# Graph attention on one core: the low part of the probabilities is taken two chunks back, the values three chunks back

## The chip, the cores and the metric

The kernel runs on 1 core of one Trainium2 chip. The metric is the device time of the launch in microseconds (us). Beside it there is one profiled execution, from which all durations come.

## What is computed

For 128 graphs of 128 nodes with 384 features, 12 heads of 32 features:

```python
h = maximum(layernorm(x), 0)
q, k, v = h @ Wq + bq, h @ Wk + bk, h @ Wv + bv          # split into 12 heads
scores = q @ k.T / sqrt(32) + beta * adj                 # per graph and head, 128 x 128
scores = where(adj > 0, scores, -9e15)
out = x + softmax(scores) @ v
```

## The kernel before

**Steps and slots.** A step takes 4 graphs (512 nodes), and there are 32. Each engine has its own instruction stream, and all five are written in the same frame: steps, and in each step 12 slots `u`. A step projects its own four graphs (q, k, v), prepares the normalised input of the next step, and does the attention of the step before. A chunk is one graph and four heads, so that a step has 12 chunks, one scored in each slot, 3 slots behind (`LAG`). A 33rd step, without projections, does what is left. The function `chunk(s, par, u, behind)` names the chunk that was scored `behind` slots ago.

**A chunk n on its way**, with the names used below:

- S: `scores` (L458), TensorE, four matmuls 128x128 into the one bank `ps_s`. It waits until B of n-1 is done.
- B: `bias_scores` (L638), VectorE, four instructions that add the mask, negate and take the row minimum (`neg_max`), each with a read of the accumulator. It waits for S, and for the exponentials of n-2, whose input it overwrites.
- E: `exps` (L523), ScalarE, four exponentials, each after its part of B.
- T: `turn_probs` (L466), TensorE, four transposes in f32 into `ps_t`, two banks in turn. It waits for E of n, and for L of n-2, which reads the same bank.
- H: `p_high` (L548), ScalarE, the transposed probabilities rounded to f16. It waits for T and for V of n-2, whose operand it overwrites.
- L: `p_low` (L644), VectorE, the bank minus H: the low part, in f16. It waits for H.
- V: `values_of` (L481 to L483), TensorE, 12 matmuls, probabilities (high and low) times values. It waits for L; with the first chunk of a graph also for the values' split on GpSimd and for a free output bank.
- After the third chunk of a graph VectorE inverts the sums (L654) and scales the output (L659), GpSimd adds x (L336), SyncE stores.

**The projections** are cut into pieces, one for each slot (`piece`, L437): q, k of 9 matmuls with 512 columns a unit, v of 9 with 384 columns, and three `turn` units (L417), transposes of the next step's input. They run over three banks. A unit's result is taken in two parts: ScalarE the high part (L543, L538, or L530 for hT) in the slot in which the unit ends, VectorE the low part (L619, or L609 for hT) in the slot after. A unit may start when the bank's earlier tenant is emptied: `bank_free`.

**The order in a slot** that scores chunk n is:

- TensorE: S(n), T(n-1), piece, V(n-2).
- ScalarE: E(n), H(n-1), high parts of the slot's units.
- VectorE: B(n), low parts of the units of the slot before, inversion, statistics (L586, L592; slots 0 and 1), scaling, mask (L598 in slot 4, L603 in slot 7), L(n-1).

The slots of the pieces, by `PIECES`: seven matmuls of q or k in slots 0, 1, 3, 4 and 7, eight in slot 2; slot 5 has turn 0 and five of k 1; slot 6 four of k 1, turn 1 and two of k 2; slot 8 turn 2 and seven of v 0; slots 9 to 11 ten, nine and ten of v. The first matmul of k 2 (slot 6) needs the bank of turn 0, thus its low part, which VectorE makes in slot 6.

Of the kernel before, what the change touches and what calls it, by code (L numbers as in the profile page):

```python
# [23 lines left out]
def graph_attention_kernel(nc, x, adj, wq, bq, wk, bk, wv, bv, beta, out):  # L24
# [6 lines left out]
    STEPS = GRAPHS // G  # L31
    TOK = G * N
    SLOTS = G * CH
    CHUNKS = STEPS * SLOTS

    LAG = CH
# [48 lines left out]
    with ExitStack() as ctx:  # L85
# [115 lines left out]
        def wait(eng, s, value):  # L201

            if value > 0:
                eng.wait_ge(s, value)
# [6 lines left out]
        def chunk(s, par, u, behind):  # L211

            v = u - LAG - behind
            back = 2 if v < 0 else 1
            n = SLOTS * (s - 1) + v
            if v >= SLOTS or (not 0 <= n < CHUNKS):
                return None
            return n, s - back, par if back == 2 else 1 - par, v % SLOTS
# [171 lines left out]
        def _(pe):  # L390
# [50 lines left out]
            def piece(s, par, u, ahead):  # L441

                for o, first, end in PIECES[u]:
                    if UNITS[o][0] != "turn":
                        project(s, par, o, first, end)
                    elif ahead:
                        bank_free(s, par, o)
                        turn(s + 1, ps_p[BANK[par][o]], UNITS[o][1])

            def scores(n, g, gp, v, odd):  # L450

                j, c = v // CH, v % CH
                if v == 0:
                    pe.wait_ge(q_in, 16 * 3 * HPC * (g + 1))
                    pe.wait_ge(k_in, 16 * 3 * HPC * (g + 1))
                wait(pe, biased_done, HPC * n)
                for i in range(HPC):
                    mm = pe.matmul(ps_s[:, i * N:(i + 1) * N], q_st[0:STACK, gp, i, c, j * N:(j + 1) * N],  # L458
                                   k_st[0:STACK, gp, i, c, j * N:(j + 1) * N], start=True, stop=True)
                mm.then_inc(scores_done, 1)  # L460

            def turn_probs(n, odd):
                pe.wait_ge(exp_done, HPC * (n + 1))
                wait(pe, p_low_done, n - 1)
                for i in range(HPC):
                    mm = pe.transpose(ps_t[odd][:, i * N:(i + 1) * N], probs[:, odd, i, :], ident[:])  # L466
                mm.then_inc(turned, 1)

            def values_of(n, g, gp, v, odd):

                j, c = v // CH, v % CH
                if c == 0:
                    wait(pe, scaled, G * g + j - 1)
                    pe.wait_ge(v_split, G * g + j + 1)
                pe.wait_ge(p_low_done, n + 1)
                for i in range(HPC):
                    h = c * HPC + i
                    o = ps_o[j % 2][:, h * VW:(h + 1) * VW]
                    high, low = pT[:, odd, 0, i, :], pT[:, odd, 1, i, :]
                    first, second = v1[:, gp, j, h, :], v2[:, gp, j, h, :]  # L480
                    pe.matmul(o, high, first, start=True, stop=False)  # L481
                    pe.matmul(o, low, first, start=False, stop=False)  # L482
                    mm = pe.matmul(o[:, 0:HD], high, second, start=False, stop=True)  # L483
                mm.then_inc(pv_done, 1)

            def step(s, par):
                proj, ahead = 0 <= s <= STEPS - 1, 0 <= s <= STEPS - 2
                for u in range(SLOTS + (LAG + 2 if s == STEPS else 0)):
                    scored, turning, valued = (chunk(s, par, u, behind) for behind in range(3))
                    if scored:  # L490
                        scores(*scored, (u - LAG) % 2)
                    if turning:
                        turn_probs(turning[0], (u - LAG - 1) % 2)
                    if proj:
                        piece(s, par, u, ahead)
                    if valued:
                        values_of(*valued, (u - LAG) % 2)

            pe.wait_ge(consts_set, 3)
            for n in range(3):  # L500
# [81 lines left out]
        def _(dve):  # L582
            def moments(s, par, j):
                wait(dve, x_in[par], 8 * (s - par) + 16)
                wait(dve, var_done, G * (s - 1) + j + 1)
                dve.bn_stats(stats[:, j, :], xs[:, par, j, :]).then_inc(stats_done, 1)  # L586
# [7 lines left out]
            def mask_unlinked(s, par):  # L594

                dve.wait_ge(adj_in, 16 * (s + 1))
                wait(dve, biased_done, HPC * SLOTS * (s - 1))
                dve.tensor_scalar(mask[:, par], adjs[:], 0.0, MASKED, ALU.is_le, ALU.mult).then_inc(unlinked, 1)  # L598
# [23 lines left out]
            def low_parts(s, par, u, ahead):  # L622

                for o in ENDED[u]:
                    if UNITS[o][0] in ("q", "k"):
                        low_part(s, par, o)
                    elif UNITS[o][0] == "turn" and ahead:
                        turn_low(s + 1, 1 - par, ps_p[BANK[par][o]], UNITS[o][1])

            def bias_scores(n, g, gp, v, odd):  # L630

                dve.wait_ge(scores_done, n + 1)
                wait(dve, exp_done, HPC * (n - 1))
                if v == 0:
                    dve.wait_ge(mask_done, g + 1)
                dve.nop(nofuse=True)
                for i in range(HPC):
                    dve.tensor_tensor_reduce(out=biased[:, odd, i, :], in0=ps_s[:, i * N:(i + 1) * N],  # L638
                                             in1=mask[:, gp, v // CH, :], scale=-1.0, scalar=3.0e38, op0=ALU.add,
                                             op1=ALU.min, accum_out=neg_max[:, odd, i:i + 1]).then_inc(biased_done, 1)  # L640

            def p_low(n, odd):
                dve.wait_ge(p_high_done, n + 1)
                dve.tensor_tensor(pT[:, odd, 1], ps_t[odd][:].rearrange("p (h q) -> p h q", q=N), pT[:, odd, 0],  # L644
                                  ALU.subtract).then_inc(p_low_done, 1)
# [4 lines left out]
            def invert_sums(g, j):  # L650

                dve.wait_ge(pv_done, CH * (G * g + j + 1))
                wait(dve, scaled, G * g + j - 1)
                dve.reciprocal(inv_sum[:, j % 2, :], outputs(j)[:, :, HD]).then_inc(inverted, 1)  # L654

            def scale_out(g, j):
                dve.wait_ge(inverted, G * g + j + 1)
                wait(dve, stored[j % 2], 16 * (G // 2 * g + j // 2))
                dve.tensor_tensor(on[:, j % 2, :].rearrange("p (h d) -> p h d", d=HD), outputs(j)[:, :, 0:HD],  # L659
                                  inv_sum[:, j % 2, :].rearrange("p (h o) -> p h o", o=1).broadcast_to([P, HEADS, HD]),  # L660
                                  ALU.mult).then_inc(scaled, 1)

            def step(s, par):
                proj, ahead = 0 <= s <= STEPS - 1, 0 <= s <= STEPS - 2
                for u in range(SLOTS + (LAG + 3 if s == STEPS else 0)):
                    scored, turning, _, valued = (chunk(s, par, u, behind) for behind in range(4))
                    ended = valued is not None and valued[3] % CH == CH - 1
                    if scored:
                        bias_scores(*scored, (u - LAG) % 2)
                    if u >= 1 and proj:  # L670
                        low_parts(s, par, u - 1, ahead)
                    if u == 0 and s >= 1:
                        low_parts(s - 1, 1 - par, SLOTS - 1, s <= STEPS - 1)
                    if ended:
                        invert_sums(valued[1], valued[3] // CH)
                    if ahead and u < 2:
                        for j in range(2 * u, 2 * u + 2):
                            moments(s + 1, 1 - par, j)
                    if ended:
                        scale_out(valued[1], valued[3] // CH)  # L680
                    if proj and u == 4:
                        mask_unlinked(s, par)
                    if proj and u == 7:
                        mask_linked(s, par)
                    if ahead and u < 2:
                        for j in range(2 * u, 2 * u + 2):
                            variance(s + 1, j)
                    if turning:
                        p_low(turning[0], (u - LAG - 1) % 2)

            for j in range(G):
                moments(0, 0, j)
# [86 lines left out]
```

## Time and profile before

| | |
|---|---|
| time, median of 3 runs | 1162.81 us (1161.45 to 1163.67) |
| profiled execution, its own time | 1164.11 us |
| its span, first to last instruction | 1162.2 us |
| TensorE (PE) busy | 1070.8 us, 92% |
| VectorE (DVE) busy | 979.4 us, 84% |
| ScalarE (ACT) busy | 892.2 us, 77% |
| GpSimd (POOL) busy | 567.8 us, 49% |
| mean granted TensorE clock | 0.976 |
| DMA | 138.79 MB, mean 119 GB/s |

The busy shares are shares of the span. Matmuls are pipelined, and each is listed with its full latency, so that TensorE's busy time holds overlaps; its real pace is read from the starts of its instructions. The same holds in a smaller way for VectorE and ScalarE, where an instruction starts some hundredths of a us before the one ahead ends. Therefore durations below are mostly differences of starts.

### The profile page before, as it was taken

What the parts mean: (1) busy time and instruction counts of PE and PEld (TensorE: products, weight loads), DVE (VectorE), ACT (ScalarE), POOL (GpSimd) and SP (SyncE); (2) the same over time, 40 slices, a digit from 0 to 9 for tenths busy, and PEclk for the clock granted to TensorE, in tenths of its full rate; (3) what the DMA queues carried; (4) which work ended last, traced back from release to release, by engine and by line L of the source; (5) the groups of instructions that cost most, each with busy time, mean ns of one, the idle gap of its engine ahead of it and who ended that gap; (6) DMA issues with size and microseconds to landing.
All of it is one profiled execution on the core that took longest, in us unless ns stands there. A gap on an engine that the chain in (4) does not pass through costs nothing. (4 is left out here: it accounts for less than half of the span.)

```text
span 1162.2 us, 33776 instructions
## 1 busy us (share of the span) xinstructions
PE 1070.8 (92%) x10959; PEld 713.0 (61%) x10959; DVE 979.4 (84%) x4343; ACT 892.2 (77%) x2343; POOL 567.8 (49%) x756
## 2 busy tenths in 40 slices
PE   4899999999999999999999999999999999999986
PEld 1366666666666666666666666666666666666654
DVE  6588988888988888898888898888889888889765
ACT  2378887778788787888787877888888878887865
POOL 3744555544455544455554445554445555444431
PEclk9999999999999999999999999999999999999965
DMA  4454434455444455444445444445544444543320
GB/s 144 118 133 122 116 101 123 126 146 137 114 104 120 120 140 147 113 123 104 115 132 146 130 122 102 118 123 139 146 114 115 110 119 130 147 129 95 98 69 28
DMA packets 91038, 138.79 MB, mean 119 GB/s; under 512 B 15600, under 2 KB 66288, under 8 KB 90864
## 3 DMA queue, kind: packets, MB, share of 16 engines
q1 hardware_dynamic: 90336, 135.85, 43.5%
q8 instruction: 88, 1.44, 0.5%
q14 instruction: 86, 0.70, 0.2%
q10 hardware_dynamic: 528, 0.79, 0.2%
HBM read 35.91 MB, written 25.17 MB: 53 GB/s over the span
## 5 line engine op out<-in xcount | busy, mean ns | idle before, releaser
L523 ACT ACTIVATE probs<-biased,neg_max 128x128 f32<-128x128 f32 x1536 | 493.5, 392 | 225.3 <-DVE neg_max L638 223.2
L437 PE MATMUL ps_p<-hT,w 128*128 128x512 f16 x1728 | 423.8, 382 | 30.1 <-DVE hT L609 22.0
L644 DVE TENSOR_TENSOR pT<-ps_t,pT 128x512 f16<-128x512 f32 x384 | 264.4, 689 | 146.9 <-ACT pT L548 143.5
L638 DVE CUSTOM_DVE_ANT_0 biased<-ps_s,mask 128x128 f32<-128x128 f32 x1536 | 351.7, 286 | 3.8 <-PE ps_s L458 2.9
L336 POOL TENSOR_TENSOR on<-on,xb 128x384 f32<-128x384 f32 x128 | 127.7, 997 | 417.7 <-DVE on L659 417.7
L466 PE MATMUL ps_t<-ident,probs 128*128 128x128 f32 x1536 | 255.0, 290 | 32.4 <-ACT probs L523 12.1
L437 PEld LDWEIGHTS ps_p<-hT,w 128*128 128x128 f16 x1728 | 166.2, 98 | 185.2 <-DVE hT L609 29.3
L548 ACT ACTIVATE pT<-ps_t 128x512 f16<-128x512 f32 x384 | 221.1, 576 | 0.7 <-PE ps_t L466 0.7
L466 PEld LDWEIGHTS ps_t<-ident,probs 128*128 128x128 f32 x1536 | 165.3, 144 | 82.8 <-ACT probs L523 81.3
L437 PE MATMUL ps_p<-w,hT 128*128 128x384 f16 x1152 | 207.6, 326 | 0.0
L481 PEld LDWEIGHTS ps_o<-v,pT 128*128 128x128 f16 x1536 | 132.2, 97 | 46.1 <-DVE pT L644 6.6
L481 PE MATMUL ps_o<-v,pT 128*128 128x33 f16 x1536 | 156.8, 179 | 3.2 <-DVE pT L644 2.3
L483 PE MATMUL ps_o<-v,pT 128*128 128x32 f16 x1536 | 155.7, 177 | 0.0
L482 PE MATMUL ps_o<-v,pT 128*128 128x33 f16 x1536 | 155.6, 178 | 0.0
L458 PE MATMUL ps_s<-k_st,q_st 96*128 96x128 f16 x1536 | 150.2, 221 | 5.4 <-DVE neg_max L638 4.3
L437 PEld LDWEIGHTS ps_p<-w,hT 128*128 128x128 f16 x1152 | 112.7, 98 | 59.7
L482 PEld LDWEIGHTS ps_o<-v,pT 128*128 128x128 f16 x1536 | 125.2, 97 | 36.7
L321 POOL TENSOR_TENSOR xb<-xs,bv_row 128x384 f32<-128x384 f32 x128 | 127.3, 1006 | 8.9 <-POOL on L336 0.4
L638 DVE DVE_READ_ACCUMULATOR2_ANT neg_max<- 128x1 f32 x1536 | 129.0, 84 | 0.0
L483 PEld LDWEIGHTS ps_o<-v,pT 128*128 128x128 f16 x1536 | 124.1, 96 | 0.0
L328 POOL CAST v<-v_f 128x384 f16<-128x384 f32 x128 | 64.8, 506 | 111.8 <-issue 102.7
L330 POOL TENSOR_TENSOR v<-v_f,v 128x384 f16<-128x384 f32 x128 | 113.6, 887 | 10.3
(62 smaller groups left out, 1044.4 us busy)
## 6 DMA issues: line engine op xcount, KB each, us to landing
q_st<-qT SPq DMA_DIRECT2D x384, 96.0 KB, 2.2
k_st<-kT SPq DMA_DIRECT2D x384, 96.0 KB, 2.2
out<-on SPq DMA_DIRECT2D x128, 192.0 KB, 2.1
xs<-in_x SPq DMA_DIRECT2D x31, 768.0 KB, 4.7
adjs<-in_adj SPq DMA_DIRECT2D x32, 256.0 KB, 4.9
xs<-in_x ACTq DMA_DIRECT2D x1, 768.0 KB, 7.3
k_st<-in_L_gnn_Wq SPq DMA_DIRECT2D x1, 576.0 KB, 5.6
k_st<-in_L_gnn_Wk SPq DMA_DIRECT2D x1, 576.0 KB, 9.4
```

The costliest lines, as they stand in the source:

```text
L321: pool.tensor_tensor(xb[:, par, j, :], xs[:, par, j, :], bv_row[:], ALU.add).then_inc(xb_done, 1)
L336: pool.tensor_tensor(on[:, j % 2, :], on[:, j % 2, :], xb[:, par, j, :], ALU.add).then_inc(added, 1)
L437: mm = pe.matmul(dst, stationary, moving, start=m == 0, stop=m == MMS - 1)
L458: mm = pe.matmul(ps_s[:, i * N:(i + 1) * N], q_st[0:STACK, gp, i, c, j * N:(j + 1) * N], k_st[0:STACK, gp, i, c, j * N:(j + 1) * N], start ...
L466: mm = pe.transpose(ps_t[odd][:, i * N:(i + 1) * N], probs[:, odd, i, :], ident[:])
L481: pe.matmul(o, high, first, start=True, stop=False)
L482: pe.matmul(o, low, first, start=False, stop=False)
L483: mm = pe.matmul(o[:, 0:HD], high, second, start=False, stop=True)
L523: act.activation(probs[:, odd, i, :], biased[:, odd, i, :], ACT.Exp, bias=neg_max[:, odd, i:i + 1], scale=-1.0).then_inc(exp_done, 1)
L548: act.activation(pT[:, odd, 0], ps_t[odd][:].rearrange("p (h q) -> p h q", q=N), ACT.Copy).then_inc(p_high_done, 1)
L638: dve.tensor_tensor_reduce(out=biased[:, odd, i, :], in0=ps_s[:, i * N:(i + 1) * N], in1=mask[:, gp, v // CH, :], scale=-1.0, scalar=3.0e3 ...
L644: dve.tensor_tensor(pT[:, odd, 1], ps_t[odd][:].rearrange("p (h q) -> p h q", q=N), pT[:, odd, 0], ALU.subtract).then_inc(p_low_done, 1)
```

## The change

On VectorE L is taken of the chunk n-2 instead of n-1, and stands directly behind B(n) instead of at the end of the slot. On TensorE V is taken of the chunk n-3 instead of n-2, and stands between S and T instead of behind the piece. ScalarE, GpSimd and SyncE keep their instructions and order. The last step has one more slot on TensorE. No buffer and no instruction is added or removed.

```diff
--- before.py
+++ after.py
@@ -485,16 +485,16 @@
 
             def step(s, par):
                 proj, ahead = 0 <= s <= STEPS - 1, 0 <= s <= STEPS - 2
-                for u in range(SLOTS + (LAG + 2 if s == STEPS else 0)):
-                    scored, turning, valued = (chunk(s, par, u, behind) for behind in range(3))
+                for u in range(SLOTS + (LAG + 3 if s == STEPS else 0)):
+                    scored, turning, valued = (chunk(s, par, u, behind) for behind in (0, 1, 3))
                     if scored:
                         scores(*scored, (u - LAG) % 2)
+                    if valued:
+                        values_of(*valued, (u - LAG - 3) % 2)
                     if turning:
                         turn_probs(turning[0], (u - LAG - 1) % 2)
                     if proj:
                         piece(s, par, u, ahead)
-                    if valued:
-                        values_of(*valued, (u - LAG) % 2)
 
             pe.wait_ge(consts_set, 3)
             for n in range(3):
@@ -663,10 +663,12 @@
             def step(s, par):
                 proj, ahead = 0 <= s <= STEPS - 1, 0 <= s <= STEPS - 2
                 for u in range(SLOTS + (LAG + 3 if s == STEPS else 0)):
-                    scored, turning, _, valued = (chunk(s, par, u, behind) for behind in range(4))
+                    scored, turned_late, valued = (chunk(s, par, u, behind) for behind in (0, 2, 3))
                     ended = valued is not None and valued[3] % CH == CH - 1
                     if scored:
                         bias_scores(*scored, (u - LAG) % 2)
+                    if turned_late:
+                        p_low(turned_late[0], (u - LAG) % 2)
                     if u >= 1 and proj:
                         low_parts(s, par, u - 1, ahead)
                     if u == 0 and s >= 1:
@@ -685,8 +687,6 @@
                     if ahead and u < 2:
                         for j in range(2 * u, 2 * u + 2):
                             variance(s + 1, j)
-                    if turning:
-                        p_low(turning[0], (u - LAG - 1) % 2)
 
             for j in range(G):
                 moments(0, 0, j)
```

TensorE, slot 9 of a middle step (S is L458, T L466, the piece L437, V L481 to L483), before:

```order
L458 MATMUL ps_s<-k_st,q_st 128x128 [waits biased_done]
L458 MATMUL ps_s<-k_st,q_st 128x128 x3
L466 MATMUL ps_t<-ident,probs 128x128 [waits p_low_done,exp_done]
L466 MATMUL ps_t<-ident,probs 128x128 x3
L437 MATMUL ps_p<-w,hT 128x384 x2
L437 MATMUL ps_p<-w,hT 128x384 [waits qk_low]
L437 MATMUL ps_p<-w,hT 128x384 x7
L481 MATMUL ps_o<-v,pT 128x33 [waits p_low_done]
L482 MATMUL ps_o<-v,pT 128x33
L483 MATMUL ps_o<-v,pT 128x32
```

The same stretch now (the nine rows left out are the rest of V):

```order
L458 MATMUL ps_s<-k_st,q_st 128x128 [waits biased_done]
L458 MATMUL ps_s<-k_st,q_st 128x128 x3
L481 MATMUL ps_o<-v,pT 128x33 [waits p_low_done,v_split,scaled]
L482 MATMUL ps_o<-v,pT 128x33
L483 MATMUL ps_o<-v,pT 128x32
...
L466 MATMUL ps_t<-ident,probs 128x128 [waits p_low_done,exp_done]
L466 MATMUL ps_t<-ident,probs 128x128 x3
L437 MATMUL ps_p<-w,hT 128x384 x2
L437 MATMUL ps_p<-w,hT 128x384 [waits qk_low]
L437 MATMUL ps_p<-w,hT 128x384 x7
```

V, with its wait for `p_low_done`, now stands behind S and ahead of T; before it stood behind the piece.

VectorE, around slot 4 of a middle step (B is L638 with its accumulator reads, L is L644, the low part of qT L619, the first mask L598), before:

```order
L644 TENSOR_TENSOR pT<-ps_t,pT 128x512 [waits p_high_done]
L638 ISA biased,neg_max<-ps_s,mask 128x128 [waits scores_done,exp_done]
L638 ISA neg_max 128x1
...
L619 SCALAR_TENSOR_TENSOR qT<-ps_p,bias_qk,qT 128x512 [waits qk_high]
L598 TENSOR_SCALAR mask<-adjs 128x512 [waits biased_done,adj_in]
L644 TENSOR_TENSOR pT<-ps_t,pT 128x512 [waits p_high_done]
L638 ISA biased,neg_max<-ps_s,mask 128x128 [waits scores_done,exp_done]
```

The same stretch now:

```order
L638 ISA biased,neg_max<-ps_s,mask 128x128 [waits scores_done,exp_done]
L638 ISA neg_max 128x1
...
L644 TENSOR_TENSOR pT<-ps_t,pT 128x512 [waits p_high_done]
L619 SCALAR_TENSOR_TENSOR qT<-ps_p,bias_qk,qT 128x512 [waits qk_high]
L598 TENSOR_SCALAR mask<-adjs 128x512 [waits biased_done,adj_in]
L638 ISA biased,neg_max<-ps_s,mask 128x128 [waits scores_done,exp_done]
```

Between two B stood the slot's other work and then L with its wait for `p_high_done`; now L stands right behind B, and nothing that waits for a fresh H stands ahead of the next B.

## Rows read from the trace of the kernel before

**Rows 1.** Waits of the whole run: in total us, how often, longest.

```profile
ACT probs L523 <- DVE neg_max L638: 223.2, 355, 2.1
...
DVE pT L644 <- ACT pT L548: 143.5, 204, 1.6
...
PEld ps_t L466 <- ACT probs L523: 81.3, 279, 1.1
```

**Rows 2.** Timeline behind the last projection: start, duration, engine, instructions, [idle before <-releaser].

```profile
1131.22 1.28 ACT L523 ACTIVATE probs<-biased,neg_max 128x128 f32<-128x128 f32 x4 [1.02 <-DVE neg_max L638]
...
1132.41 0.58 ACT L548 ACTIVATE pT<-ps_t 128x512 f16<-128x512 f32 x1
...
1133.02 0.69 DVE L644 TENSOR_TENSOR pT<-ps_t,pT 128x512 f16<-128x512 f32 x1 [1.26 <-ACT pT L548]
1133.63 0.28 DVE L638 CUSTOM_DVE_ANT_0 biased<-ps_s,mask 128x128 f32<-128x128 f32 x1
...
1134.01 1.28 ACT L523 ACTIVATE probs<-biased,neg_max 128x128 f32<-128x128 f32 x4 [1.02 <-DVE neg_max L638]
...
1135.35 1.11 PE L466 MATMUL ps_t<-ident,probs 128*128 128x128 f32 x4
```

**Rows 3.** Timeline, TensorE over a slot without a wait.

```profile
618.51 0.38 PE L458 MATMUL ps_s<-k_st,q_st 96*128 96x128 f16 x4
618.74 0.61 PE L466 MATMUL ps_t<-ident,probs 128*128 128x128 f32 x4
619.18 1.67 PE L437 MATMUL ps_p<-hT,w 128*128 128x512 f16 x7
...
620.69 0.18 PE L481 MATMUL ps_o<-v,pT 128*128 128x33 f16 x1
...
620.99 0.38 PE L458 MATMUL ps_s<-k_st,q_st 96*128 96x128 f16 x4
```

**Rows 4.** Timeline, VectorE's kinds of work, and the groups by line: the first mask.

```profile
602.98 1.02 DVE L586 BATCH_NORM_STATS2 stats<-xs 128x6 f32<-128x384 f32 x2
...
604.33 0.69 DVE L644 TENSOR_TENSOR pT<-ps_t,pT 128x512 f16<-128x512 f32 x1
...
604.94 0.28 DVE L638 CUSTOM_DVE_ANT_0 biased<-ps_s,mask 128x128 f32<-128x128 f32 x1
...
605.78 0.75 DVE L619 SCALAR_TENSOR_TENSOR qT<-ps_p,bias_qk,qT 128x512 f16<-128x512 f32 x1
...
606.44 0.22 DVE L654 RECIPROCAL inv_sum<-ps_o 128x12 f32<-128x12 f32 x1
...
607.17 0.68 DVE L644 TENSOR_TENSOR pT<-ps_t,pT 128x512 f16<-128x512 f32 x1
...
620.59 0.68 DVE L609 SCALAR_TENSOR_TENSOR hT<-ps_p,hT 128x512 f16<-128x512 f32 x1
621.18 0.74 DVE L603 SCALAR_TENSOR_TENSOR mask<-adjs,beta_col,mask 128x512 f32<-128x512 f32 x1
621.84 0.69 DVE L644 TENSOR_TENSOR pT<-ps_t,pT 128x512 f16<-128x512 f32 x1
...
L598 DVE TENSOR_SCALAR mask<-adjs 128x512 f32<-128x512 f32 x32 | 14.2, 444 | 0.0
```

**Rows 5.** Timeline, low part of hT and the projection that waits for it.

```profile
617.02 0.69 DVE L609 SCALAR_TENSOR_TENSOR hT<-ps_p,hT 128x512 f16<-128x512 f32 x1
...
617.77 0.60 PE L437 MATMUL ps_p<-hT,w 128*128 128x512 f16 x2 [0.74 <-DVE hT L609]
```

**Rows 6.** Timeline, the first chunk.

```profile
58.05 0.38 PE L458 MATMUL ps_s<-k_st,q_st 96*128 96x128 f16 x4 [1.02 <-DMA k_st<-kT]
...
58.62 0.29 DVE L638 CUSTOM_DVE_ANT_0 biased<-ps_s,mask 128x128 f32<-128x128 f32 x1 [2.88 <-PE ps_s L458]
...
58.96 1.28 ACT L523 ACTIVATE probs<-biased,neg_max 128x128 f32<-128x128 f32 x4 [2.06 <-DVE neg_max L638]
```

**Rows 7.** Stretch behind the last projection: busy us of each engine, PEclk, DMA share, GB/s.

```profile
1130.00:1162.00 32.00, 21.46 (x204) 14.23 (x203) 18.05 (x91) 16.68 (x47) 4.78 (x5) 0.50 0.09 32
```


## The prediction

> **What bounds the kernel now.** I read the waits first [rows 1]. ScalarE waits 223.2 us before E for VectorE's row minimum, VectorE 143.5 us before L for H, and TensorE's weight loads 81.3 us, 279 times, before T for E. Three engines that wait for each other in a ring: the question is which ring closes. The timeline behind the last projection shows it bare [rows 2]. E starts at 1131.22, H at 1132.41, L at 1133.02, the next B at 1133.63, the next E at 1134.01: E 1.19, H 0.61, L 0.61, first part of B 0.38, in sum 2.79 us a chunk, each starting when the one ahead lets it. E(n-1), H(n-2), L(n-2), B(n), E(n): the only reason for the step from L to B is VectorE's order, since B reads nothing that L writes. TensorE has little to do there and the period is still 2.79, so it is a ring of ScalarE and VectorE alone.
>
> With projections the same ring holds. The first E starts at 58.96 [rows 6]; the E at 1131.22 [rows 2] is 375 chunks later. Six of these are behind the last projection, at 2.79; the other 369 take 1072.26 - 16.7 = 1055.5 us, 2.86 each, or 34.33 a step. TensorE's own pace is lower. In a slot without a wait S takes 0.23, T 0.44, seven matmuls of 512 columns 1.51 (0.216 each, so 0.162 for 384 columns) and V 0.30 [rows 3]; a turn is four f32 transposes like T, 0.44. With the pieces of the 12 slots: 2.48 in slots 0, 1, 3, 4, 7; 2.70 in 2 and 6; 2.49 in 5; 2.54, 2.59, 2.43, 2.59 in 8 to 11. Sum 30.44 a step, 3.9 less than the step takes. I call that TensorE's floor.
>
> VectorE's work, by starts [rows 4]: B 0.84 (604.94 to 605.78), L 0.61, a low part of q or k 0.66, of hT 0.59, inversion with scaling 0.73, statistics 1.35, masks 0.44 and 0.66. By slot 0 to 11: 2.80, 2.80, 2.84, 2.11, 2.55, 2.84, 2.04, 3.36, 2.84, 2.04, 1.45, 2.18; sum 29.85. So its mean is just under TensorE's, but in six slots it has more to do.
>
> **The change, part by part.** Nothing is removed or added, so the work stays 30.44 and 29.85.
>
> 1. L out of the way of B. B(n) now waits for S(n) and for VectorE's other work. The link L to B of the ring is gone; L(n-2) comes after B(n), a full slot after H(n-2), so it should not wait: the 143.5 us should all but vanish, and so should most of the 223.2.
>
> 2. V between S and T. It gives E 0.30 us more before T needs it, but V itself is now needed at 0.23 into the slot, and T, the piece and the next S are queued behind it. V(n-3) needs L(n-3), which VectorE makes in the slot before, behind B. H(n-1) waits for V(n-3), which stands ahead of T(n-1) anyway: no new cost.
>
> 3. What TensorE then waits for. I lay the slots out. B starts 0.57 after S at the earliest [rows 6]; V is released 0.84 + 0.75 after B starts (0.75 is from the start of a 512-column VectorE instruction to the matmul that waits for it [rows 5]); T is released 0.38 + 1.34 after B starts (the 1.34 is E at 1134.01 to T at 1135.35 [rows 2]). TensorE's slot starts at 0 in slot 0, VectorE's B at 0.57. VectorE's B then starts behind TensorE's slot by 0.57, 0.89, 1.21, 1.35, 0.98, 0.82, 1.17 in slots 0 to 6. V waits where the lag in the slot before, plus 1.59, passes that slot's length plus 0.23: only in slot 4, by 0.23 (1.35 + 1.59 = 2.94 against 2.71). In slot 6 k 2 needs hT's low part, now behind B and L: 1.17 + 1.45 + 0.75 = 3.37 after the slot's start, against 2.27 where TensorE gets there. Wait 1.10. Before, it was 0.74 by the row [rows 5]. This wait lets VectorE catch up: lag 0.57 in slot 7, 1.45 in 8 (slot 7 has 3.36 of work), 1.75 in 9, 0.93 in 10, 0.57 in 11. V waits 0.27 in slot 9 and 0.25 in slot 10. T's condition (lag + 1.72 against the slot's length + 0.53) is never the later one. A step is 30.44 + 0.23 + 1.10 + 0.27 + 0.25 = 32.29 us.
>
> 4. The sum. 34.33 - 32.29 = 2.04 a step, times 369/12 = 30.75 steps: 62.7 us. The last step with projections has no turns and no statistics: TensorE needs 3 x 0.44 less and the wait of 1.10 is gone, while its old pace is the ring's 2.79; I put 2 us more.
>
> 5. Behind the last projection, 15 chunks at 2.79. TensorE is at the granted clock 0.50 there, 1.2 GHz [rows 7], so S, V and T cost at most twice the 0.97 of [rows 3]: 1.94. VectorE needs (3 x 1.45 + 0.73)/3 = 1.69, ScalarE 1.19 + 0.48 (E, and H when it doesn't wait) = 1.67. Between 1.69 and 1.94 and nearer the upper, since V waits for L and the scaling comes in bursts: 1.9. Gain 15 x 0.89 = 13.3. The Trainium skill (TensorE: Matmul & The Clock Gate, Part 1) says that activity releases TensorE's throttle. The row agrees that the clock is low where TensorE is sparse; by that rule the denser tail could stay at 2.4 GHz, and then VectorE's 1.69 would hold and the total be 3 us lower. I keep the 0.50 of the row.
>
> The extra slot on TensorE costs nothing: the last V waits for the last L either way.
>
> What no row shows is the handing over from V's short matmuls to T's f32 weight loads. The nearest rows are S to T, 0.23 with nothing added, and T's start after a wait. Below nothing is excluded by in-order work; above I take 0.05 a slot, 0.6 a step, 18 us. I take 0 and keep 18 for the range.
>
> Sum: 62.7 + 2 + 13.3 = 78 us off the profiled execution's 1164.1, which gives 1086; the median of the runs is 1.3 lower, so **1085**.
>
> **Rivals.**
>
> - **TensorE's floor.** If VectorE's real lag is smaller than my sums (0.57 was read once, at the first chunk), V never waits and only hT's wait of 1.10 stays: 31.54 a step, 2.79 x 30.75 + 15 = 101 off, **1062**. For it: V's three waits are small. Against: six slots of VectorE are longer than TensorE's.
> - **No slack between the engines.** If each slot costs the longer of the two engines, 2.80, 2.80, 2.84, 2.48, 2.55, 2.84, 2.70, 3.36, 2.84, 2.59, 2.43, 2.59 = 32.82, with hT's wait 33.92 a step: 0.41 x 30.75 + 15 = 28 off, **1135**. For it: V at the slot's head has only L's slack. Against: S needs B only by the slot's end, 0.3 us after B is done even at lag 1.35. A part of this rival, and the 18 us above, are the way to the upper end.
> - **Slower: V's wait becomes the ring.** V(n), T(n+2) 0.44, piece 1.51, S to B 0.57, B 0.84, L to V 0.75, with V's 0.30: 4.41 us from V(n) to V(n+2), two chunks, plus what VectorE has to do ahead of B(n+4). It decides from 2 x 2.86 = 5.72 up, when 1.31 more lies ahead. The mean other work of a slot is (29.85 - 12 x 1.45)/12 = 1.04, giving 5.45; the longest, slot 7's, is 1.91, giving 6.32. If every second pair met that, a chunk took 2.94, 0.08 x 369 = 30 more, less 13 for the tail: **1181**. Against: 1.91 comes once a step.
> - **No change.** The two buffers of pT and ps_t are the true bound, and the wait moves from L to V and H. The Trainium skill (Perfetto Trace Analysis, Identifying Performance Opportunities) says that a bubble that repeats can mean too few buffers; no buffer is added here. Against: the rows name another engine's result, and the ring of [rows 2] closes through the order alone. **1163**.
>
> **Chances.** Forecast 0.60 (alone: 1070 to 1102), floor 0.17, no slack 0.15, slower 0.04, no change 0.04. Range 1060 to 1116: the floor with its small variations is in, of the no-slack case the milder half. A difference under 0.2% (2.3 us) can't be told from none. Faster 0.92, same 0.04, slower 0.04.
>
> **What the profile after should show.** L's wait for H near nothing; E's wait for the row minimum well under half of 223; T's wait for E nearly gone, and in its place V waiting for L in slots 4, 9 and 10, some 90 times by 0.2 to 0.3; hT's wait in slot 6 longer, near 1.1; 32.3 us between like points of two steps; under 2 us a chunk behind the last projection. Wrong it would be if VectorE still idled over 1 us a slot, if V waited in most slots, or if a wait for k_st's or q_st's transfer, with less time now, appeared at a step's first S.

## The result, and the profile after

The changed kernel takes 1079.64 us (median of 4 runs, 1078.93 to 1080.68); the kernel before 1162.28 us in the same comparison. The ratio is 0.9289, 95% interval 0.9273 to 0.9305. Forecast were 1085 us, range 1060 to 1116.

| | before | after |
|---|---|---|
| span of the profiled execution | 1162.2 us | 1077.4 us |
| TensorE busy | 1070.8 us, 92% | 1020.8 us, 95% |
| VectorE busy | 979.4 us, 84% | 967.6 us, 90% |
| ScalarE busy | 892.2 us, 77% | 884.5 us, 82% |
| mean granted TensorE clock | 0.976 | 0.992 |

The work is the same; the span is 84.8 us shorter. First the waits of the whole run after (waiter, whom for, total us, times, longest):

```profile
ACT probs L523 <- DVE neg_max L638: 115.5, 217, 1.4
DVE biased L638 <- PE ps_s L458: 74.5, 100, 1.7
...
PEld ps_p L437 <- DVE hT L609: 26.1, 31, 1.1
...
PEld ps_o L481 <- DVE pT L644: 5.9, 15, 1.2
...
DVE pT L644 <- ACT pT L548: 0.9, 1, 0.9
...
PEld ps_t L466 <- ACT probs L523: 0.3, 1, 0.3
```

These answer to [rows 1]. VectorE's wait for H fell from 143.5 us to 0.9, so L no longer waits. T's wait for E fell from 81.3 us to 0.3. ScalarE's wait for the row minimum is 115.5 us, half of the 223.2: it is not a bound now, only the time that ScalarE has over. VectorE waits for S instead, 74.5 us (2.9 before): in the light slots it has caught up with TensorE.

One step, on TensorE (start, duration, operation; slot 2, S of slot 3, then slots 6, 9 and 10, then slot 2 of the next step):

```profile
599.81 0.39 PE L458 MATMUL ps_s<-k_st,q_st 96*128 96x128 f16 x4
...
600.34 0.64 PE L466 MATMUL ps_t<-ident,probs 128*128 128x128 f32 x4
600.81 1.89 PE L437 MATMUL ps_p<-hT,w 128*128 128x512 f16 x8
602.54 0.39 PE L458 MATMUL ps_s<-k_st,q_st 96*128 96x128 f16 x4
...
610.09 0.39 PE L458 MATMUL ps_s<-k_st,q_st 96*128 96x128 f16 x4
...
611.95 0.60 PE L417 MATMUL ps_p<-ident,hn 128*128 128x128 f32 x4
613.17 0.61 PE L437 MATMUL ps_p<-hT,w 128*128 128x512 f16 x2 [0.62 <-DVE hT L609]
...
618.71 0.39 PE L458 MATMUL ps_s<-k_st,q_st 96*128 96x128 f16 x4
619.23 0.18 PE L481 MATMUL ps_o<-v,pT 128*128 128x33 f16 x1
...
621.62 0.39 PE L458 MATMUL ps_s<-k_st,q_st 96*128 96x128 f16 x4
621.97 0.19 PE L481 MATMUL ps_o<-v,pT 128*128 128x33 f16 x1
...
631.87 0.39 PE L458 MATMUL ps_s<-k_st,q_st 96*128 96x128 f16 x4
```

VectorE's B in slots 3, 6 and 9 of the same step:

```profile
603.63 0.28 DVE L638 CUSTOM_DVE_ANT_0 biased<-ps_s,mask 128x128 f32<-128x128 f32 x1
...
610.99 0.28 DVE L638 CUSTOM_DVE_ANT_0 biased<-ps_s,mask 128x128 f32<-128x128 f32 x1
...
620.38 0.28 DVE L638 CUSTOM_DVE_ANT_0 biased<-ps_s,mask 128x128 f32<-128x128 f32 x1
```

From S of slot 2 at 599.81 to the next at 631.87 are 32.06 us, where 34.33 were. TensorE reaches k 2 (the last projection unit of slot 6, behind turn 1) at 611.95 + 0.44 = 612.39 and waits until 613.17, 0.78 us. V starts 0.52 after S in slot 9 (618.71 to 619.23) and 0.35 after in slot 10, where 0.22 is the pace without a wait: waits of 0.30 and 0.13. T to the piece is 0.47 (600.34 to 600.81), not the 0.44 of [rows 3]. B starts 1.09 behind S in slot 3 (602.54 to 603.63), 0.90 in slot 6 (610.09 to 610.99) and 1.67 in slot 9 (618.71 to 620.38).

Where the 84.8 us are, by the exponentials. After: the first chunk, the first behind the last projection, and the fourteenth after that.

```profile
58.42 1.28 ACT L523 ACTIVATE probs<-biased,neg_max 128x128 f32<-128x128 f32 x4 [0.88 <-DVE neg_max L638]
...
1043.11 1.28 ACT L523 ACTIVATE probs<-biased,neg_max 128x128 f32<-128x128 f32 x4
...
1068.39 1.28 ACT L523 ACTIVATE probs<-biased,neg_max 128x128 f32<-128x128 f32 x4
```

Before, where the first chunk is in [rows 6]:

```profile
1114.49 1.28 ACT L523 ACTIVATE probs<-biased,neg_max 128x128 f32<-128x128 f32 x4 [0.27 <-DVE neg_max L638]
...
1153.53 1.28 ACT L523 ACTIVATE probs<-biased,neg_max 128x128 f32<-128x128 f32 x4 [1.02 <-DVE neg_max L638]
```

369 chunks took 1055.5 us and take 984.7 (58.42 to 1043.11, 32.02 a step): 70.8 us. The next 14 took 39.04 and take 25.28: 13.8 us. The rest, 0.2, is at the two ends.

### The profile page after: what moved, and what is told of

The parts are those of the page before. It is cut to its first block and busy times, and to the rows that moved or that the text cites. A ratio compares the mean times of both kernels' runs of the same rounds, so it can differ in the third digit from the quotient of the medians.

```text
span 1077.4 us, 33776 instructions
## 1 busy us (share of the span) xinstructions
PE 1020.8 (95%) x10959; PEld 709.7 (66%) x10959; DVE 967.6 (90%) x4343; ACT 884.5 (82%) x2343; POOL 567.5 (53%) x756
## 5 line engine op out<-in xcount | busy, mean ns | idle before, releaser
L523 ACT ACTIVATE probs<-biased,neg_max 128x128 f32<-128x128 f32 x1536 | 490.5, 390 | 146.9 <-DVE neg_max L638 115.5
L437 PE MATMUL ps_p<-hT,w 128*128 128x512 f16 x1728 | 423.5, 382 | 23.9 <-DVE hT L609 18.7
L638 DVE CUSTOM_DVE_ANT_0 biased<-ps_s,mask 128x128 f32<-128x128 f32 x1536 | 353.5, 286 | 75.8 <-PE ps_s L458 74.5
L437 PEld LDWEIGHTS ps_p<-hT,w 128*128 128x128 f16 x1728 | 167.5, 98 | 175.7 <-DVE hT L609 26.1
L644 DVE TENSOR_TENSOR pT<-ps_t,pT 128x512 f16<-128x512 f32 x384 | 263.3, 686 | 0.9 <-ACT pT L548 0.9
L466 PE MATMUL ps_t<-ident,probs 128*128 128x128 f32 x1536 | 245.4, 283 | 0.1
L437 PE MATMUL ps_p<-w,hT 128*128 128x384 f16 x1152 | 207.6, 326 | 0.0
L458 PEld LDWEIGHTS ps_s<-k_st,q_st 96*128 96x128 f16 x1536 | 117.5, 97 | 81.3 <-DVE neg_max L638 6.9
L481 PE MATMUL ps_o<-v,pT 128*128 128x33 f16 x1536 | 157.1, 179 | 8.9 <-DVE pT L644 5.2
L466 PEld LDWEIGHTS ps_t<-ident,probs 128*128 128x128 f32 x1536 | 161.7, 141 | 0.3 <-ACT probs L523 0.3
L483 PE MATMUL ps_o<-v,pT 128*128 128x32 f16 x1536 | 155.2, 177 | 0.0
L458 PE MATMUL ps_s<-k_st,q_st 96*128 96x128 f16 x1536 | 149.4, 219 | 3.7 <-DVE neg_max L638 2.4
L437 PEld LDWEIGHTS ps_p<-w,hT 128*128 128x128 f16 x1152 | 112.7, 98 | 59.7
L481 PEld LDWEIGHTS ps_o<-v,pT 128*128 128x128 f16 x1536 | 130.1, 96 | 20.5 <-issue 10.7
L638 DVE DVE_READ_ACCUMULATOR2_ANT neg_max<- 128x1 f32 x1536 | 127.5, 83 | 0.3
L483 PEld LDWEIGHTS ps_o<-v,pT 128*128 128x128 f16 x1536 | 123.7, 96 | 0.0
```

What stands on the lines that cost most here:

```text
L437: mm = pe.matmul(dst, stationary, moving, start=m == 0, stop=m == MMS - 1)
L523: act.activation(probs[:, odd, i, :], biased[:, odd, i, :], ACT.Exp, bias=neg_max[:, odd, i:i + 1], scale=-1.0).then_inc(exp_done, 1)
```

## The experiments

Each kernel is the changed one or the one before, with one thing altered. Times are medians; ratios are to the kernel before, run beside it on the same chip (1161.65 us beside the values behind the transposes, the changed kernel once more and the operation in slot 7; 1161.53 beside the first four; 1161.40 beside the other four).

### The two moves apart, and the two places

**The values alone.** VectorE's stream is that of the kernel before, TensorE's that of the changed kernel.

```diff
-                    scored, turned_late, valued = (chunk(s, par, u, behind) for behind in (0, 2, 3))
+                    scored, turning, _, valued = (chunk(s, par, u, behind) for behind in range(4))
...
-                    if turned_late:
-                        p_low(turned_late[0], (u - LAG) % 2)
...
+                    if turning:
+                        p_low(turning[0], (u - LAG - 1) % 2)
```

> The values alone are moved (three chunks back, between scores and transposes); VectorE keeps the low part of the last chunk at the end of its slot, so the ring of ScalarE and VectorE (exponentials, high part, low part, next masked scores: 2.79 us a chunk) is whole. Theory (the order of VectorE was the bound): about 1162 us, within 6, still 2.79 us a chunk behind the last projection, and VectorE still waits some 140 us for the high part. Rival (the gain came from the 0.30 us that the values give the exponentials before the transposes need them): under 1120 us.

Measured: 1157.96 us, ratio 0.9969 (0.9958 to 0.9981). The ring is whole, and so is the time, all but 3.6 us: the rival is out. Its exponentials behind the last projection (ScalarE, timeline):

```profile
1124.88 1.28 ACT L523 ACTIVATE probs<-biased,neg_max 128x128 f32<-128x128 f32 x4 [1.03 <-DVE neg_max L638]
...
1127.67 1.28 ACT L523 ACTIVATE probs<-biased,neg_max 128x128 f32<-128x128 f32 x4 [1.02 <-DVE neg_max L638]
```

Three of its waits:

```profile
DVE pT L644 <- ACT pT L548: 142.0, 204, 1.5
...
PEld ps_s L458 <- DVE neg_max L638: 95.1, 260, 1.6
...
PEld ps_t L466 <- ACT probs L523: 3.7, 8, 1.1
```

Still 2.79 us a chunk, and 142.0 us of L waiting for H. T's wait for E did vanish (3.7 us, from 81.3), just as the 0.30 us of V ahead of it would have it, and TensorE waits 95.1 us at S for B instead (5.7 before). A wait of TensorE that disappears tells nothing if the ring that made it doesn't run through TensorE.

**The low part alone.** VectorE's stream is the changed one, TensorE's that of the kernel before.

```diff
-                for u in range(SLOTS + (LAG + 3 if s == STEPS else 0)):
-                    scored, turning, valued = (chunk(s, par, u, behind) for behind in (0, 1, 3))
+                for u in range(SLOTS + (LAG + 2 if s == STEPS else 0)):
+                    scored, turning, valued = (chunk(s, par, u, behind) for behind in range(3))
...
-                    if valued:
-                        values_of(*valued, (u - LAG - 3) % 2)
                     if turning:
                         turn_probs(turning[0], (u - LAG - 1) % 2)
                     if proj:
                         piece(s, par, u, ahead)
+                    if valued:
+                        values_of(*valued, (u - LAG) % 2)
```

> The low part alone is moved behind the masked scores, of the chunk but one back; the values keep their place behind the piece and are of two chunks back, so they need a low part that VectorE makes in the same slot. Theory: the ring is broken, but TensorE now waits at the end of its slot (lag of VectorE + 0.84 + 0.75 against 2.18), by hand 33.5 us a step against 32.06 now, and 2.46 us a chunk behind the last projection against 1.8: about 1134 us. Rival (the move of VectorE's low part is all of the change, the values' move a detail): within 10 us of 1080.

Measured: 1130.08 us, ratio 0.9732 (0.9703 to 0.9760). So 31 us come from moving L alone, which takes the link from L to B out of the ring, and the other 51 of the whole change from where V stands. The rival, within 10 us of 1080, is out. By its exponentials the 369 chunks take 1022.6 us, 32.9 less than before, but the 14 behind the last projection only 1.0 less (38.04 us, 2.72 each, where 2.46 were forecast): there V waits for L of its own slot, and the next S stands behind V. V is now the instruction that waits:

```profile
PEld ps_o L481 <- DVE pT L644: 98.7, 226, 1.6
...
PE ps_o L481 <- DVE pT L644: 40.0, 53, 1.3
```

**The low part at the end of VectorE's slot**, of the chunk but one back as in the change.

```diff
-                    if turned_late:
-                        p_low(turned_late[0], (u - LAG) % 2)
...
                             variance(s + 1, j)
+                    if turned_late:
+                        p_low(turned_late[0], (u - LAG) % 2)
```

> As the changed kernel, but VectorE takes the low part (of the chunk but one back, as changed) at the end of its slot, not behind the masked scores. If only the distance to the high part matters (rival), the ring is broken all the same and it stays within 10 us of 1080. Theory of the lags: the values at the head of TensorE's slot need this low part 0.14 us after the end of VectorE's slot, so that a slot takes VectorE's work + 0.48 us wherever that is longer: 36.4 us a step, about 1210 us, slower than before.

Measured: 1160.27 us, ratio 0.9990 (0.9979 to 1.0001): in sum the gain is gone, though the ring is broken (of L's wait for H only 1.0 us is left, once). The rival is out; the theory's direction is right and its size wrong, 1210 forecast. The head of slot 8 (TensorE's S and V, VectorE's L and B):

```profile
626.70 0.39 PE L458 MATMUL ps_s<-k_st,q_st 96*128 96x128 f16 x4
...
627.52 0.68 DVE L644 TENSOR_TENSOR pT<-ps_t,pT 128x512 f16<-128x512 f32 x1
...
628.12 0.28 DVE L638 CUSTOM_DVE_ANT_0 biased<-ps_s,mask 128x128 f32<-128x128 f32 x1
...
628.25 0.19 PE L481 MATMUL ps_o<-v,pT 128*128 128x33 f16 x1 [1.17 <-DVE pT L644]
```

V stands 1.55 us behind S (626.70 to 628.25), and starts 0.73 after L does. My sum charged each of VectorE's long slots to TensorE in full. But a slot that V has made longer gives VectorE that time back: the wait in slot t + 1 is VectorE's end of slot t + 0.14, less the start of slot t + 1, less 0.23, with the wait of slot t in that start. Done so, with the prediction's own numbers, a step has 3.98 us of waits and takes 34.42; the trace has 34.63 in the mean of the 369 chunks (59.50 to 1124.49). The unchanged time hides two parts, by the first exponential behind the last projection and the fourteenth after it:

```profile
1124.49 1.28 ACT L523 ACTIVATE probs<-biased,neg_max 128x128 f32<-128x128 f32 x4
...
1150.51 1.27 ACT L523 ACTIVATE probs<-biased,neg_max 128x128 f32<-128x128 f32 x4
```

The 369 chunks take 1065.0 us, 9.5 more than before; the next 14 take 26.02, 13.0 less. So the broken ring shows where VectorE has little other work, and in the steps L's late place takes it back.

**The values behind the piece**, of three chunks back as in the change.

```diff
-                    if valued:
-                        values_of(*valued, (u - LAG - 3) % 2)
                     if turning:
                         turn_probs(turning[0], (u - LAG - 1) % 2)
                     if proj:
                         piece(s, par, u, ahead)
+                    if valued:
+                        values_of(*valued, (u - LAG - 3) % 2)
```

> As the changed kernel, but TensorE takes the values of three chunks back behind the piece instead of between scores and transposes. The values then never wait for the low part (0.43 us a step won), but the high part waits for them until TensorE's slot ends, ScalarE's high parts and the next exponentials stand behind it, and the transposes lose 0.30 us of slack: by hand 0.5 to 0.8 us a step more, about 1100 us. Rival (the place within the slot is free, only the distance counts): 1066 to 1075 us.

Measured: 1104.61 us, ratio 0.9512 (0.9485 to 0.9540). Of the 51 us, then, the greater distance of V gives 25 and its place in the slot the other 25. The rival (1075 at most) is out. H now waits for V, since V reads the buffer that H overwrites, and T waits behind that:

```profile
ACT pT L548 <- PE ps_o L483: 110.6, 198, 1.5
...
...
PEld ps_t L466 <- ACT probs L523: 34.6, 97, 0.8
```

**The values behind the transposes.**

```diff
-                    if valued:
-                        values_of(*valued, (u - LAG - 3) % 2)
                     if turning:
                         turn_probs(turning[0], (u - LAG - 1) % 2)
+                    if valued:
+                        values_of(*valued, (u - LAG - 3) % 2)
                     if proj:
```

> As the changed kernel, but the values of three chunks back stand behind the transposes, ahead of the piece. They no longer wait for the low part (0.43 us a step), but the transposes are 0.30 us earlier in the slot and wait for the exponentials where VectorE is late: by the lags of the changed kernel's trace 0.07 in slot 4, 0.33 in slot 9, 0.2 in slot 10. Theory: about 0.2 us a step more, 1080 to 1088 us. Rival (the values' wait for the low part is the dearer of the two): 1066 to 1074 us.

Measured: 1084.50 us, ratio 0.9335 (0.9320 to 0.9351); the changed kernel beside it gave 0.9293 (0.9279 to 0.9306). So the place ahead of T is worth 5 us, and the rival is out. T and V in slot 7 of a middle step, where neither waits:

```profile
616.75 0.61 PE L466 MATMUL ps_t<-ident,probs 128*128 128x128 f32 x4
...
617.19 0.18 PE L481 MATMUL ps_o<-v,pT 128*128 128x33 f16 x1
```

Behind S, as in the kernel before, T takes 0.44 (616.75 to 617.19); directly behind V, in the changed kernel, it takes 0.47.

**The changed kernel once more.**

> The changed kernel once more, on the chip of the two runs above: 1079.6 us, within 2.

Measured: 1079.39 us.

### Is VectorE the bound, and where?

**An operation more in slot 10, and in slot 7**, read by nobody:

```diff
                     if turned_late:
                         p_low(turned_late[0], (u - LAG) % 2)
+                    if proj and u == 10:
+                        dve.tensor_tensor(spare[:], b_row[:], b_row[:], ALU.add)
```

The counterpart has `u == 7`. Both allocate the tile `spare`, 128x768 in f32.

> The changed kernel with one idle VectorE operation more in slot 10 of each step (the bias rows, 768 columns, added to themselves into a spare tile, read by nobody; about 0.8 us). VectorE waits 0.83 us for scores there. Theory of the lags (VectorE isn't the bound as a whole, only in the slots after its long ones): it costs under 0.1 us a step, 1079 to 1083 us. Rival (VectorE, at 90% busy, is the bound): 0.8 us a step, 1104 us. The same operation in slot 7 is to follow as its counterpart.

> The same idle VectorE operation as before (768 columns), now in slot 7, VectorE's longest. In slot 10 it took 1.45 us in the one place read and cost nothing. Theory of the lags: here it makes VectorE late for slots 8 and 9 and shows in full as TensorE's waits, its own duration a step (0.8 us without company of GpSimd, up to 1.45): 25 to 45 us more, 1104 to 1125 us. Rival (VectorE's work has slack wherever it stands): under 1085 us.

Measured: 1079.64 us (ratio 0.9293, 0.9275 to 0.9312) in slot 10, 1106.38 us (0.9524, 0.9509 to 0.9538) in slot 7. The operation itself, by its tile (count, then the least, the median and the greatest duration in ns), in slot 10:

```profile
L674 DVE TENSOR_TENSOR spare<-b_row x32: 948/1444/1544, 47.9 to 1039.9; 128x768 f32<-128x768 f32 x32
```

and in slot 7:

```profile
L674 DVE TENSOR_TENSOR spare<-b_row x32: 946/948/951, 43.1 to 1057.3; 128x768 f32<-128x768 f32 x32
```

In slot 10 its median is 1444 ns and it costs nothing that can be told (the interval is 2 us either way); in slot 7 it is 948 ns long and costs 27.0 us, 0.87 in each of 31 steps. VectorE at 90% busy is no bound as a whole, and is the bound in the slots behind its longest one.

**hT's low part first in slot 6.**

```diff
-                    if turned_late:
+                    if turned_late and not (proj and u == 6):
                         p_low(turned_late[0], (u - LAG) % 2)
                     if u >= 1 and proj:
                         low_parts(s, par, u - 1, ahead)
+                    if turned_late and proj and u == 6:
+                        p_low(turned_late[0], (u - LAG) % 2)
```

> As the changed kernel, but in slot 6 VectorE takes hT's low part ahead of the low part of the probabilities. In the changed kernel's trace the first matmul of k 2 waits for it 0.78 us in every step (612.39 to 613.17). Theory (VectorE's order in this slot alone makes that wait): hT's low part comes 0.60 earlier, the wait falls to about 0.2, 0.59 us a step less, 1062 us. Rival (the wait lets VectorE catch up, and its going brings longer waits of the values in slots 7 to 10): within 4 us of 1080.

Measured: 1061.46 us, ratio 0.9135 (0.9119 to 0.9150), as the theory had it.

**The second mask operation in slot 6.**

```diff
-                    if proj and u == 7:
+                    if proj and u == 6:
                         mask_linked(s, par)
```

> The changed kernel with the second mask operation in slot 6 instead of 7, nothing else. The values wait for the low part 0.30 us in slot 9 and 0.13 us in slot 10 of each step. Theory: that is the lag from slot 7, VectorE's longest (3.36 us); with 2.70 us both waits go: 13 us less, 1066 us. Rival (these waits come from slot 8's own 2.84 us, or don't matter): 1076 us or more.

Measured: 1067.39 us, ratio 0.9187 (0.9173 to 0.9201), within 2 us of the theory's 1066.

**Both.**

> hT's low part first in slot 6, and the second mask operation (0.66 us) in slot 6 instead of 7, where VectorE stood idle for 1.06 us. Theory of the lags: the gains of both parts add up, since they act on different waits (0.59 us a step in slot 6, 0.43 in slots 9 and 10): about 1049 us. Rival (slot 6 has no room for both, VectorE comes late into slot 7): 1060 us or more.

Measured: 1049.64 us, ratio 0.9035 (0.9022 to 0.9048), the fastest of all. The gains, 18 and 12 us, add up to the 30. A step on TensorE: S of slot 9 in one step and in the next, and between them the end of turn 1 and k 2 in slot 6.

```profile
601.09 0.39 PE L458 MATMUL ps_s<-k_st,q_st 96*128 96x128 f16 x4
...
625.99 0.60 PE L417 MATMUL ps_p<-ident,hn 128*128 128x128 f32 x4
626.61 0.61 PE L437 MATMUL ps_p<-hT,w 128*128 128x512 f16 x2
...
632.14 0.39 PE L458 MATMUL ps_s<-k_st,q_st 96*128 96x128 f16 x4
```

31.05 us from S to S (slot 9 at 601.09 and 632.14). Of hT's wait 0.18 is left (625.99 + 0.44 = 626.43 to 626.61), and of V's none. With T's 0.47, TensorE's floor is 30.44 + 12 x 0.03 = 30.8, so only 0.25 us of a step is waiting.

## Why the prediction was right

The forecast of 1085 us was 5 above the time, and the mechanism is the one that it named. That it came so near is in part luck: a step's waits were 0.64 us shorter than forecast (1.21 for 1.85), and the handing over to T, which the prediction put at nothing, cost 0.36 a step. Point by point:

1. **L out of the way of B.** Right. The ring's period was 2.79 us and L's wait for H fell from 143.5 to 0.9 us. The values alone left both as they were; the low part alone gained 31 us. The rival "no change", that two buffers are the bound, is out: no buffer was added.
2. **V between S and T, a chunk later.** Right that it is needed and that it costs H nothing there (no wait of H for V is in the list of the changed kernel, 110.6 us are with V behind the piece): its distance gives 25 us, its place another 25 against the end of the slot, of which the place behind T has 20.
3. **A step of 32.29 us**; measured 32.06 by TensorE's S, 32.02 in the mean of 369 chunks. Term by term: hT's wait 0.78 instead of 1.10; none in slot 4 instead of 0.23; 0.30 instead of 0.27 in slot 9; 0.13 instead of 0.25 in slot 10; and 0.03 more for each T, 0.36 a step or 11 us in all. In sum 0.28 less, 32.01. The last is the handing over from V's matmuls to T's weight loads, which the prediction named, took as 0 and kept 18 us for in its range; with V behind T it is gone, so it is V's place that makes it. The mis-sized term is VectorE's lag ahead of slot 7: B behind S is 1.09 in slot 3 where 1.35 was forecast, so that V does not wait in slot 4, and 0.90 in slot 6 where 1.17 was; after hT's wait it is near (slot 9: 1.67 for 1.75). Part of it is T's 0.03, by which each of TensorE's slots is longer; the rest is VectorE's work in slots 0, 1 and 4, which by the starts of B is 0.1 less in each than the sums of [rows 4]. Those sums also put seven slots of VectorE above TensorE's (0, 1, 2, 4, 5, 7 and 8), where the prediction counted six. All this made 70.8 us saved up to the last projection where 62.7 + 2 were forecast.
4. **Behind the last projection**: 13.8 us saved (14 chunks) where 13.3 (15 chunks) were forecast, but not as told. The clock was not 0.50. A stretch of the changed kernel behind the last projection, and its end (busy us of each engine, granted clock, DMA share, GB/s):

```profile
1045.00:1060.00 15.00, 10.84 (x163) 7.59 (x161) 14.30 (x80) 13.71 (x42) 3.83 (x5) 1.00 0.17 54
1060.00:1077.00 17.00, 9.75 (x140) 7.43 (x140) 11.78 (x56) 10.38 (x30) 3.32 (x4) 0.69 0.13 47
```

The same stretches in the second profiled execution of this kernel:

```profile
1045.00:1060.00 15.00, 12.08 (x160) 9.00 (x158) 13.35 (x72) 13.23 (x40) 3.15 (x4) 0.77 0.17 54
1060.00:1077.00 17.00, 9.22 (x147) 6.55 (x144) 12.78 (x63) 10.96 (x32) 3.98 (x4) 0.85 0.13 47
```

And the kernel before, right behind its last projection:

```profile
1114.40:1130.00 15.60, 12.09 (x117) 8.02 (x115) 9.69 (x55) 10.39 (x30) 3.54 (x6) 0.54 0.11 34
```

In the first execution the clock stayed at 1.00, 2.4 GHz, through the first stretch and fell in the second; in the repeat it was 0.77 and 0.85, and the 14 chunks took 26.02 us instead of 25.28. Both are above the 0.50 that I took from [rows 7]. All 13 profiled executions divide in the same way. Over the 14 chunks the clock is 0.51 in the kernel before (2.79 us a chunk), 0.53 with the values alone (2.78) and 0.54 with the low part alone (2.72); in the ten others, at 1.75 to 1.86 us a chunk, it is 0.87 to 1.00. The Trainium skill's rule (TensorE: Matmul & The Clock Gate, Part 1) that activity releases the throttle fits these rows better than my 0.50. That the denser order is the cause is argued from them: no run alters the one without the other. At one place the first S of the last graphs waited for a transfer:

```profile
1045.27 0.40 PE L458 MATMUL ps_s<-k_st,q_st 96*128 96x128 f16 x4
...
1048.02 0.38 PE L458 MATMUL ps_s<-k_st,q_st 96*128 96x128 f16 x4 [1.19 <-DMA k_st<-kT]
```

That is 1.19 us, once; it is the wait for k_st that the prediction's last paragraph named as a sign of being wrong, and it is too short to matter. Without it 14 chunks would take 24.1 us, 1.72 each, close to VectorE's 1.69.

5. **The rivals.** TensorE's floor (1062) and no slack (1135) were the two sides of VectorE's lag, and kernels beyond both were built: with two VectorE operations placed better the kernel runs at 1049.64, under the floor as I had it, since hT's wait of 1.10 was counted into it; with L at the slot's end, where V finds it at the last moment, it is at 1160.27. "V's wait becomes the ring" did not happen: V's waits are 0.43 us a step. "No change" is answered in 1.
6. **The signs.** V waited in slots 9 and 10 and not in slot 4; the list of waits names 15 at V's weight loads and 17 at its matmuls, and the others are seen only in the distance from S to V. hT's wait did not grow to 1.1: the profile labels it 0.62, where [rows 5] had 0.74. By starts it is 0.78, where it was 0.90 before (616.43 + 0.44 to 617.77), and it is this 0.90 that the forecast 1.10 should have been set against. ScalarE's wait for the row minimum stayed at half, not well under it.

Not settled: why the values alone give 3.6 us. Their gap to the kernel before is clear of noise. By the exponentials it lies in the steps (34.14 us each for 34.33) and not behind them (38.95 us for 39.04), and most of it between E of slot 6 and E of slot 7 (2.78 us for 2.90 in the median), where V of slot 6 no longer stands between k 2 with its wait and the next S; no run takes it apart further. Nor was L's distance tried alone: in the run with L at the end of the slot V stood at the head of TensorE's, where it needs L soonest. L at the end with V behind the piece was not run.

## What to carry to other kernels

Follow the waits until they close into a ring, and look in it for a link that is there by the order of an engine's stream and not by data. That link can be moved: no buffer and no faster instruction was needed here. Where an engine's result is taken a slot later, put its maker at the head of the slot and its taker where enough has passed, since here the same shift with the maker at the slot's end gave nothing in sum. Then lay out, slot by slot, by how much the second busiest engine is late: the same operation cost 27 us in one slot and nothing in another, and taking one operation first and another a slot earlier, where the engine stood idle, gave 30 us.

## What was not expected of the hardware

The spare operation on VectorE, 768 columns with two SBUF inputs, took 948 ns in each of 32 executions in slot 7 and 1444 ns in the median in slot 10 (948 to 1544). In slot 10 GpSimd was splitting values (timeline of GpSimd and VectorE; the first execution, and one from the middle):

```profile
47.88 0.95 DVE L674 TENSOR_TENSOR spare<-b_row 128x768 f32<-128x768 f32 x1
48.42 0.78 POOL L329 CAST v<-v_f 128x384 f16<-128x384 f32 x1 [5.74 <-ACT v_f L539]
...
624.35 0.89 POOL L331 TENSOR_TENSOR v<-v_f,v 128x384 f16<-128x384 f32 x1
624.60 1.45 DVE L674 TENSOR_TENSOR spare<-b_row 128x768 f32<-128x768 f32 x1
```

In 31 of the 32 in slot 10 the operation starts while GpSimd's `TENSOR_TENSOR` runs, and it ends 0.81 to 0.82 us after that one's end, whether it met the last 0.51 us of it (1323 ns), 0.63 (1444) or 0.73 (1544). GpSimd's operation keeps its 0.88 us. The one execution that met none of it took 948 ns; there GpSimd's `CAST` began behind it and took 0.78 us, where its mean in the changed kernel is 0.51. In slot 7 none of the 32 met an operation of GpSimd, and all took 946 to 951 ns. So the two don't share the time: whichever came second waited for the other, VectorE for most of what was left of GpSimd's operation. No run took GpSimd's work away from slot 10.

The clock behind the last projection is the other: with the same instructions in a denser order it was 0.96 and 0.87 over the 14 chunks, in two executions of one kernel, instead of 0.51.
